# Softmax weights divided ahead of their transpose with the values stationary, and the MLP's centring and first products in high and low parts

## The chip, the core and the metric

The kernel runs on one core of a Trainium2 chip. The metric is the time on the device from start to end of one execution, in microseconds (us), as the median of several runs. The engines that matter are TensorE (matmuls and transposes; its weight loads run beside them), VectorE, ScalarE, GpSimd, and SyncE, which issues DMAs. Each engine takes its instructions strictly in the order in which they are written for it. They wait for one another only through semaphores.

## The reference

Three blocks in a row, each on a layer norm of `x` (4 sequences of 512 tokens, 128 features): softmax attention A, a two-layer block with local attention and an MLP (`ffn`), a linear attention B, and `ffn` again. The change lies in `ffn`. Cut to what matters:

```python
def _layer(x, wqkv, qs, ksc, wo, lg, lb, w1, b1, w2, b2):
    h = shift_token(x)                       # the upper 64 features come from the token before
    q, k, v = jnp.split(h @ wqkv, 3, axis=-1)   # 8 heads of 64
    q = l2norm(q) * qs
    k = l2norm(k) * ksc
    q, k = rotary_xpos(q, k)
    o = local_attention(q, k, v)             # windows of 64; each looks at itself and the one before
    x = x + o @ wo
    h = shift_token(x)
    mu = h.mean(-1, keepdims=True)
    var = h.var(-1, keepdims=True)
    h = (h - mu) / jnp.sqrt(var + 1e-05) * lg + lb
    h = h @ w1 + b1
    a, g = jnp.split(h, 2, axis=-1)          # 341 each
    h = a * jax.nn.gelu(g, approximate=False)
    return x + h @ w2 + b2
...
x = x + attn_a(_layernorm(x)); x = x + ffn(_layernorm(x)); x = x + attn_b(_layernorm(x)); x = x + ffn(_layernorm(x))
```

## The kernel before

Attention A is a program of its own (`attention_a`, the first 249 us). All that follows is `stream`: one pipeline over 64 tiles of 128 tokens (2 calls of `ffn`, 2 layers, 4 sequences, 4 tiles each). Four tiles make a group, that is one sequence in one layer; there are 16 groups.

The order on each engine is written out by the table `STEP`. In step s an engine goes through its list, and a stage with lag L works on tile s - L in that step (`of_tile`), or on a group once in four steps (`of_group`), or on a sequence of attention B between the two calls (`of_sequence`). So a row's place in the list and its lag decide what stands ahead of what. The four steps of a group hold different group work: after the group's last tile, wo comes 3 steps later, the centring and the variance 4, w1 5, w2 6. So each of the four steps of a group has one of these. On TensorE the centring and w1 stand ahead of the masks of the scores, the variance, w2 and wo behind them.

For one tile, in the order of the data: `project` (TensorE, L1157 to L1159: q, k and v, each as three products of high and low parts in the type fp32r); `squares` (ScalarE, L1368); `rope` (VectorE, four operations at L1521 and L1525 into `A` and `BS`, then the reduction of the squares, L1532); `norm` (ScalarE) and `scale` (GpSimd, L1086 and L1091); `turn` (TensorE transposes q and k, L1167) and its copies (ScalarE, L1388 and L1392); `scores` (TensorE, masks at L1180, products at L1195); the row maxima (VectorE, `soften`, L1557); the exponentials (ScalarE, `soften`, eight of 128x128 into `PW`, L1402); `turn_p` (TensorE, transposes of `PW`, L1205) and the two copies into `PT` (one on ScalarE, L1424, one on VectorE, L1549); `sums` (TensorE, L1216): the transposed weights stand still and the values `V` and `VS`, with a column of ones for the sum of the weights, are moved through; the division (VectorE, L1564 and L1568, into `ON`); `turn_o` (TensorE, transposes of `ON`, L1228) and its copy into `OT` (ScalarE, L1433). Then, once a group: `wo` (TensorE, L1255; VectorE adds at L1574; GpSimd shifts into `mid`, L1106 to L1110), the centring (L1273) and the variance (L1279) as FP32 products on TensorE with ScalarE's square, logarithm and exponential (L1446, L1453, L1456) and VectorE's two operations into `mid` (L1583, L1587), `w1` (TensorE, six FP32 products, L1286; ScalarE's gelu; VectorE at L1603), `w2` (TensorE, L1294; VectorE at L1613, or L1620 and L1624).

The 8 banks of PSUM go round in the order in which TensorE's stages take them: `take(kind, i)` waits until the bank's occupant of eight places earlier has been read (`FREED`).

Of the kernel before, what the change touches and what calls it, by code (L numbers as in the profile page):

```python
# [858 lines left out]
def of_first(k):  # L859
# [6 lines left out]
           ("project", 0, of_tile), ("features_b", 10, of_sequence), ("turn", 1, of_tile), ("context", 9, of_sequence),  # L866
           ("turn_o", 3, of_tile), ("project_b", 10, of_sequence), ("w1", 5, of_group), ("turn_p", 2, of_tile), ("turn_p_2", 2, of_tile),
# [3 lines left out]
           ("var_y", 10, of_sequence), ("w2", 6, of_group), ("wo", 3, of_group), ("sums", 2, of_tile), ("store", 6, of_end)],  # L871
    "ACT": [("features_a", 0, of_first), ("latent", 8, of_sequence),
            ("squares", 0, of_tile), ("features_b", 10, of_sequence), ("turn", 1, of_tile), ("values", 0, of_tile), ("turn_o", 3, of_tile),
            ("center_mlp", 4, of_group), ("center_a", 2, of_first), ("center_b", 7, of_sequence),
            ("center_y", 10, of_sequence), ("split", SEQS, of_tile), ("w1", 5, of_group), ("turn_p", 2, of_tile), ("keys_b", 8, of_sequence),
            ("norm", 0, of_tile), ("var_mlp", 4, of_group), ("var_a", 2, of_first), ("var_b", 7, of_sequence),
            ("var_y", 10, of_sequence), ("soften", 1, of_tile), ("store", 6, of_end)],
    "DVE": [("lead", 0, of_lead), ("project_a", 1, of_first), ("latent", 8, of_sequence), ("rope", 0, of_tile), ("context", 9, of_sequence), ("project_b", 10, of_sequence),
            ("w1", 5, of_group), ("turn_p_2", 2, of_tile), ("keys_b", 8, of_sequence), ("soften", 1, of_tile),
            ("tokens_b", 9, of_sequence), ("var_mlp", 4, of_group), ("var_a", 2, of_first),  # L880
            ("var_b", 7, of_sequence), ("var_y", 10, of_sequence), ("wo", 3, of_group),
            ("w2", 6, of_group), ("sums", 2, of_tile)],
    "POOL": [("lead", 0, of_lead), ("split", SEQS, of_tile), ("scale", 0, of_tile), ("w2", 6, of_group),
# [23 lines left out]
def stream(nc, a, g, out):  # L907

    psum, X, Y, eps, cst, cstb = g.psum, g.X, g.Y, g.eps, g.cst, g.cstb
    norms, number = number_norms()  # L910

    order = []
    for stage, i in engine_plan("PE"):
# [4 lines left out]
        elif stage in ("scores", "sums", "keys_b", "tokens_b"):  # L918
# [5 lines left out]
        elif stage == "latent":  # L924
            order += [("latent", i), ("query_b", i)]
        elif stage[:7] == "center_":
            order += [("center", number[stage[7:], i])]
        elif stage[:4] == "var_":
            order += [("var", number[stage[4:], i])]
        elif stage in ("turn_o", "wo", "w2", "context", "features_b", "project_b", "store", "features_a", "project_a"):  # L930
            order += [(stage, i)]
    at = {x: i for i, x in enumerate(order)}

    def bank(kind, i):
# [7 lines left out]
             "sums": ("divided", lambda i: i + 1), "turn_o": ("o_copied", lambda i: i + 1),  # L942
# [17 lines left out]
    with ExitStack() as ctx:  # L960
# [8 lines left out]
        w1 = sb("w1", [P, LAYERS, 2 * HID])  # L969
# [14 lines left out]
        V = sb("V", [P, 4, HW, DW + 1])  # L984
        VS = sb("VS", [P, 4, HW, DW + 1])
# [3 lines left out]
        RD = sb("RD", [P, 4, PAIRS])  # L989
        ON = sb("ON", [P, 4, PAIRS, DW])  # L990
        OT = sb("OT", [P, PAIRS, T])
        mid = sb("mid", [P, T])
        ln_squared = sb("ln_squared", [P, T])
        LR = sb("LR", [P, T])
        gates = sb("gates", [P, 3, T])
        hidden = sb("hidden", [P, 3, T])
# [11 lines left out]
        OUT = sb("OUT", [P, 2, 4, P])  # L1008

        def pieces():  # L1010

            todo = []
            for layer in range(LAYERS):
                def row(name):
                    return a[name][layer:layer + 1]

                by_head = row("L0_ffn_wo").rearrange("a (cc c j d) n -> c d (a cc) j n", cc=2, c=2, j=2)
                todo += [
                    *((wo[DW * c:DW * c + DW, layer, 2 * cc:2 * cc + 2, :], by_head[c, :, cc])
                      for c in range(2) for cc in range(2)),  # L1020
# [16 lines left out]
        with block:  # L1037
            @block.sync
            def _(sp):
# [3 lines left out]
                sp.wait_ge(s("zeroed"), 3)  # L1043
                for stage, k in engine_plan("SP"):
                    if stage == "values":

                        sp.wait_ge(s("v_copied"), k + 1)
                        if k >= 4:
                            sp.wait_ge(s("sums"), 2 * k - 6)
# [15 lines left out]
            def _(pool):  # L1065
                nc.gpsimd.memset(KT[:, :, 2 * TILES - 1, :], 0.0).then_inc(s("zeroed"), 1)
                nc.gpsimd.memset(VS[0:WIN, :, :, :], 0.0).then_inc(s("zeroed"), 1)
                nc.gpsimd.memset(V[:, :, :, DW:DW + 1], 1.0).then_inc(s("zeroed"), 1)
# [4 lines left out]
                nc.gpsimd.memset(mid[64:P, 0:1], 0.0).then_inc(s("mid_zero"), 1)  # L1073
                pool.wait_ge(s("mid_zero"), 1)
# [7 lines left out]
                for stage, i in engine_plan("POOL"):  # L1082
                    if stage == "scale":
# [8 lines left out]
                            .then_inc(s("scaled"), 1)  # L1092
# [611 lines left out]
```

## Time and profile before

| | before |
|---|---|
| median of 3 runs | 1003.37 us (1003.19 to 1005.01) |
| the profiled execution | 1004.09 us, of it the span of the core 1002.3 us |
| TensorE busy (weight loads apart) | 941.9 us, 94% |
| VectorE, ScalarE busy | 737.2 us, 74%; 730.1 us, 73% |
| GpSimd busy | 384.0 us, 38% |
| granted TensorE clock, mean | 0.991 |

The busy times are sums over the whole span, and matmuls overlap one another in the records, so that a start-to-start distance tells more of their price than a duration does. Idle time is shown with what ended it. A wait for several semaphores is put down to the last. The granted clock is given as a share of full speed, so that 0.50 is the lower level.

### The profile page before, as it was taken

The numbers are of one execution on the slowest core, as the hardware profiler recorded it, in microseconds if no ns is written. First come the engines' busy times: TensorE is split into PE (matmuls) and PEld (weight loads), VectorE is DVE, ScalarE is ACT, GpSimd is POOL, SyncE is SP. The second block draws the span as 40 slices with busy tenths as digits, with TensorE's granted clock in tenths as the row PEclk, the third lists the DMA queues.
The fourth block names the chain that finished last, engine by engine and source line by source line (L and its number), as shares of the span: only waits on it lengthen the run. The fifth ranks groups of instructions, "written<-read, shape, count | busy, mean of one in ns | idle before, by whom it ended". The sixth has DMA issues, their size and how long they took to land.

```text
span 1002.3 us, 22947 instructions
## 1 busy us (share of the span) xinstructions
PE 941.9 (94%) x8744; PEld 577.3 (58%) x8744; DVE 737.2 (74%) x1225; ACT 730.1 (73%) x1564; POOL 384.0 (38%) x266
## 2 busy tenths in 40 slices
PE   8999999998889999999999999999999999999985
PEld 4333333333566676666766566666666766667652
DVE  6887878883887777777777677777677777777741
ACT  3577777777687786877867677777777868788652
POOL 2110113101666535455443534444365354544501
PEclk9999999999899999999999999999999999999997
DMA  2200000000411101011000101000011010110100
GB/s 82 66 8 2 2 1 2 2 1 2 122 29 28 24 18 33 18 28 23 18 23 17 23 18 23 17 17 18 18 27 24 18 33 18 27 35 17 44 12 10
DMA packets 23303, 23.72 MB, mean 24 GB/s; under 512 B 8626, under 2 KB 15068, under 8 KB 23196
## 3 DMA queue, kind: packets, MB, share of 16 engines
q1 hardware_dynamic: 23196, 22.27, 9.3%
q8 instruction: 71, 1.16, 0.5%
q14 instruction: 36, 0.29, 0.1%
HBM read 6.16 MB, written 1.05 MB: 7 GB/s over the span
## 4 chain that ended last, share of the span: by engine, by line
PE 54%; DVE 11%; ACT 5%; issue 3%; POOL 2%; DVEq 0%; POOLq 0%
PE psum L1286 8%; PE psum L1255 6%; PE psum L1195 5%; PE psum L1294 4%; PE psum L1216 4%; PE psum L1205 3%; PE psum L1167 3%; PE psum L1157 3%; DVE f_BS L1525 3%; PE psum L1279 3%; DVE f_A L1521 3%; PE psum L1159 3%; PE psum L1158 3%; PE psum L1273 2%; PE psum L1180 2%
## 5 line engine op out<-in xcount | busy, mean ns | idle before, releaser
L1086 POOL TENSOR_TENSOR f_A<-f_A,f_BS 128x1024 f32<-128x1024 f32 x64 | 151.1, 2362 | 201.1 <-DVE f_BS L1525 200.9
L765 DVE TENSOR_REDUCE a_M<-psum 128x2 f32<-128x1024 f32 x128 | 155.4, 1221 | 33.4 <-PE psum L560 32.6
L1091 POOL TENSOR_TENSOR f_A<-f_A,f_RN 128x1024 f32<-128x1024 f32 x64 | 121.8, 1903 | 90.0 <-ACT f_RN L1417 86.1
L1402 ACT ACTIVATE f_PW<-psum,f_NM 128x128 f32<-128x128 f32 x512 | 138.9, 382 | 16.4 <-DVE f_NM L1557 16.4
L683 ACT ACTIVATE a_PT<-psum 128x1024 f32<-128x1024 f32 x128 | 128.6, 1023 | 23.5 <-PE psum L570 23.4
L1521 DVE TENSOR_TENSOR f_A<-psum,cos 128x512 f32<-128x512 f32 x128 | 87.7, 685 | 37.7 <-ACT f_SQ L1368 37.6
L1368 ACT ACTIVATE f_SQ<-psum 128x512 f32<-128x512 f32 x128 | 74.5, 624 | 49.7 <-PE psum L1159 46.8
L1557 DVE TENSOR_REDUCE f_NM<-psum 128x4 f32<-128x512 f32 x128 | 82.2, 684 | 32.7 <-PE psum L1195 32.7
L1286 PE MATMUL psum<-f_mid,f_w 128*128 128x512 f32 (+1 forms) x192 | 87.4, 605 | 2.7 <-DVE f_mid L1587 2.7
L1525 DVE TENSOR_TENSOR f_BS<-psum,sin 128x512 f32<-128x512 f32 x128 | 87.2, 681 | 0.0
L1216 PEld LDWEIGHTS psum<-f_VS,f_PT 128*64 128x64 f32 x1024 | 64.5, 137 | 38.8 <-issue 37.5
L492 PE MATMUL psum<-a_PT,a_VA 128*12 128x256 f32 x1024 | 79.4, 383 | 0.2 <-ACT a_PT L683 0.2
L1532 DVE TENSOR_REDUCE f_SS<-f_SQ 128x16 f32<-128x1024 f32 x64 | 77.4, 1209 | 0.0
L1216 PE MATMUL psum<-f_VS,f_PT 128*64 128x65 f32 x1024 | 73.3, 225 | 0.7 <-DMA f_VS<-f_V 0.5
L1167 PE MATMUL psum<-const,f_A 128*128 128x128 f32 x512 | 66.6, 273 | 7.4 <-POOL f_A L1091 7.4
L1216 PE MATMUL psum<-f_V,f_PT 128*64 128x65 f32 x1024 | 73.3, 225 | 0.0
L1167 PEld LDWEIGHTS psum<-const,f_A 128*128 128x128 f32 x512 | 59.3, 140 | 17.0 <-POOL f_A L1091 9.5
L1195 PE MATMUL psum<-f_KT,f_QT 64*64 64x128 f32 x2048 | 68.2, 271 | 0.4 <-ACT f_KT L1392 0.4
L1205 PE MATMUL psum<-const,f_PW 128*128 128x128 f32 x512 | 67.1, 273 | 1.0 <-DVE f_BS L1525 1.0
L1205 PEld LDWEIGHTS psum<-const,f_PW 128*128 128x128 f32 x512 | 58.5, 141 | 12.4 <-issue 12.4
L1216 PEld LDWEIGHTS psum<-f_V,f_PT 128*64 128x64 f32 x1024 | 64.5, 137 | 0.0
L1195 PEld LDWEIGHTS psum<-f_KT,f_QT 64*64 64x64 f32 x2048 | 61.6, 134 | 4.8 <-ACT f_KT L1392 0.7
(196 smaller groups left out, 1936.2 us busy)
## 6 DMA issues: line engine op xcount, KB each, us to landing
f_VS<-f_V SPq DMA_DIRECT2D x112, 130.0 KB, 2.3
raw<-L_ffn_wqkv_dram SPq DMA_DIRECT2D x2, 768.0 KB, 5.8
a_XT<-L_attn_a_x_dram SPq DMA_DIRECT2D x4, 256.0 KB, 2.9
out_dram<-f_OUT SPq DMA_DIRECT2D x4, 256.0 KB, 2.3
f_w<-L_ffn_w_dram SPq DMA_DIRECT2D x2, 341.0 KB
tables<-const_dram SPq DMA_DIRECT2D x1, 512.0 KB, 3.7
f_wo<-L_ffn_wo_dram SPq DMA_DIRECT2D x8, 64.0 KB
const<-const_dram SPq DMA_DIRECT2D x1, 264.0 KB, 3.0
```

Of the source, the lines that this page charges most:

```text
L683: nc.scalar.activation(PT[:, i % 4, :, :], psum[:, pair("by_key", i), :], ACT.Exp, scale=float(DA) ** -0.5).then_inc(s("exped"), 1)
L765: nc.vector.tensor_reduce(M[:, quads % 2, t, 2 * j:2 * j + 2], psum[:, pair("scores", i), :], AX_X, ALU.max).then_inc(s("maxed"), 1)
L1086: nc.gpsimd.tensor_tensor(A[:, k % 2, :, :], A[:, k % 2, :, :], BS[:, k % 2, :, :], ALU.add)\
L1091: nc.gpsimd.tensor_tensor(x, x, RN[:, k % 2, :, None].to_broadcast([P, 2 * HW, DW]), ALU.mult)\
L1167: last = nc.tensor.transpose(dst[:, P * c:P * c + P], A[:, k % 2, w, P * c:P * c + P], g.ident)
L1195: last = nc.tensor.matmul(dst[j][WIN * w:WIN * w + WIN, P * c:P * c + P].rearrange("p (s x) -> p s x", s=2), QT[rows, k % 2, c, WIN * w:WI ...
L1205: last = nc.tensor.transpose(dst[:, P * c:P * c + P], PW[:, u % 4, c, :], g.ident)
L1216: last = nc.tensor.matmul(dst[WIN * w:WIN * w + WIN, c, :], PT[:, u % 4, c, WIN * w:WIN * w + WIN], values[:, k % 4, 2 * c + j, :], start= ...
L1286: nc.tensor.matmul(take(kind, 3 * i + blk)[0:w, :], w1[:, layer, first + lo:first + lo + w], mid[:, :], start=True, stop=True).then_inc(s( ...
L1402: last = nc.scalar.activation(PW[:, u % 4, c, :], psum[:, bank("scores", u), P * c:P * c + P], ACT.Exp, bias=NM[:, u % 4, c:c + 1])
L1521: nc.vector.tensor_tensor(A[:, k % 2, w, :].rearrange("p (h d) -> p h d", d=DW), x.rearrange("p (h d) -> p h d", d=DW), g.cos[:, layer, t, ...
L1525: nc.vector.tensor_tensor(BS[:, k % 2, w, :].rearrange("p (h s d) -> p h s d", s=2, d=DW // 2), x.rearrange("p (h s d) -> p h s d", s=2, d ...
```

## The change

There are two parts that do not depend on each other.

**Attention.** The exponentials in `PW` are summed by VectorE (a reduction over each 128, both halves of the tile at once), the reciprocals are taken, and GpSimd multiplies `PW` by them: the new stage `weigh`, lag 2, ahead of `rope` on VectorE and of `scale` on GpSimd. The transposes `turn_p` wait for that and go from lag 2 to 3, one ahead of `turn` and one behind it. In `sums` the values now stand still and the weights are moved through, so that the result comes out transposed: the ones column, the division on VectorE, `ON` and `turn_o` go, and ScalarE copies the result of `sums` straight into `OT`. `sums` has lag 3 and stands ahead of the centring and of `scores`, where before it was the last stage but one of a step. The copy L1549 on VectorE keeps its place behind `rope`, with lag 3.

**MLP.** `mid` becomes a high part `mid_h` and a low part `mid_l` (fp32r). GpSimd makes both; the centring is two products in place of one FP32 product; each of the six first products is three. VectorE makes the two parts of the normalized input with one more operation. The weights w1 and the centring matrix are split once, at step 4 on ScalarE (`split_w1`) and step 5 on GpSimd. `wo` is loaded in another layout, in 2 transfers in place of 8.

```diff
-           ("turn_o", 3, of_tile), ("project_b", 10, of_sequence), ("w1", 5, of_group), ("turn_p", 2, of_tile), ("turn_p_2", 2, of_tile),
+           ("project", 0, of_tile), ("features_b", 10, of_sequence), ("turn_p", 3, of_tile), ("turn", 1, of_tile), ("context", 9, of_sequence),
+           ("turn_p_2", 3, of_tile), ("project_b", 10, of_sequence), ("w1", 5, of_group), ("sums", 3, of_tile),
...
+    "DVE": [("lead", 0, of_lead), ("project_a", 1, of_first), ("latent", 8, of_sequence), ("weigh", 2, of_tile), ("rope", 0, of_tile), ("turn_p_2", 3, of_tile),
...
+                    elif stage == "weigh":
+                        k = i
+                        pool.wait_ge(s("den_recip"), k + 1)
+                        x = PW[:, 2 * (k % 2):2 * (k % 2) + 2, :, :].rearrange("p u c x -> p (u c) x")
+                        nc.gpsimd.tensor_tensor(x, x, RD[:, k % 2, :, None].to_broadcast([P, 2 * PAIRS, P]), ALU.mult)\
+                            .then_inc(s("weighed"), 1)
...
                 def turn_p(u):
-                    pe.wait_ge(s("exped"), u + 1)
+                    pe.wait_ge(s("weighed"), u // 2 + 1)
...
                 def sums(k):
                     pe.wait_ge(s(f"moved{k % 4}"), moved(k))
-                    for j in range(2):
-                        u = 2 * k + j
-                        pe.wait_ge(s(("p_copied", "p_copied_2")[j]), k + 1)
...
-                                    dst[WIN * w:WIN * w + WIN, c, :], PT[:, u % 4, c, WIN * w:WIN * w + WIN],
-                                    values[:, k % 4, 2 * c + j, :], start=True, stop=True)
...
+                    pe.wait_ge(s("v_copied"), k + 1)
+                    dst = take("sums", k).rearrange("p (c x) -> p c x", c=PAIRS)
+                    pe.wait_ge(s("p_copied"), k + 1)
+                    pe.wait_ge(s("p_copied_2"), k + 1)
+                    for c in range(PAIRS):
+                        for w, values in ((0, VS), (1, V)):
+                            for j in range(2):
                                 last = nc.tensor.matmul(
+                                    dst[DW * j:DW * j + DW, c, WIN * w:WIN * w + WIN],
+                                    values[:, k % 4, 2 * c + j, :],
+                                    PT[:, (2 * k + j) % 4, c, WIN * w:WIN * w + WIN], start=True, stop=True)
+                    last.then_inc(s("sums"), 1)
...
+                        if use == "mlp":
+                            nc.tensor.matmul(dst, centre[:, :], mid_h[:, :], start=True, stop=False)
+                            last = nc.tensor.matmul(dst, centre[:, :], mid_l[:, :], start=False, stop=True)
...
+                                nc.tensor.matmul(dst, w1_h[:, layer, of], mid_h[:, :], start=True, stop=False)
+                                nc.tensor.matmul(dst, w1_h[:, layer, of], mid_l[:, :], start=False, stop=False)
+                                nc.tensor.matmul(dst, w1_l[:, layer, of], mid_h[:, :], start=False, stop=True)\
+                                  .then_inc(s(kind), 1)
...
+                    elif stage == "weigh":
+                        k = i
+                        dve.wait_ge(s("exped"), 2 * k + 2)
+                        if k >= 2:
+                            dve.wait_ge(s("weighed"), k - 1)
+                        x = PW[:, 2 * (k % 2):2 * (k % 2) + 2, :, :].rearrange("p u c x -> p (u c) x")
+                        nc.vector.tensor_reduce(RD[:, k % 2, :], x, AX_X, ALU.add).then_inc(s("den"), 1)
+                        dve.wait_ge(s("den"), k + 1)
+                        nc.vector.reciprocal(RD[:, k % 2, :], RD[:, k % 2, :]).then_inc(s("den_recip"), 1)
...
+                            nc.vector.scalar_tensor_tensor(out=mid_l[:, :], in0=ln_squared[:, :],
+                                                           scalar=vecs[:, layer, 1:2], in1=mid_h[:, :].bitcast(F32),
+                                                           op0=ALU.add, op1=ALU.subtract).then_inc(s("ln_done"), 1)
```

What this does to the order, on VectorE first, between the maxima (`f_NM`) of one tile and those of the next, in a step of wo. Before:

```order
L1557 TENSOR_REDUCE f_NM<-psum 128x4 x2
L1574 TENSOR_TENSOR Y<-Y,psum 128x512
L1564 RECIPROCAL f_RD<-psum 128x4
L1568 TENSOR_TENSOR f_ON<-psum,f_RD 128x256
L1564 RECIPROCAL f_RD<-psum 128x4
L1568 TENSOR_TENSOR f_ON<-psum,f_RD 128x256
L1521 TENSOR_TENSOR f_A<-psum,cos 128x512
L1525 TENSOR_TENSOR f_BS<-psum,sin 128x512
L1521 TENSOR_TENSOR f_A<-psum,cos 128x512
L1525 TENSOR_TENSOR f_BS<-psum,sin 128x512
L1532 TENSOR_REDUCE f_SS<-f_SQ 128x16
L1549 COPY f_PT<-psum 128x512
```

And the same stretch of the changed kernel (its L1577 is the old L1557, L1592 the old L1574, L1569 the old L1549):

```order
L1577 TENSOR_REDUCE f_NM<-psum 128x4 x2
L1592 TENSOR_TENSOR Y<-Y,psum 128x512
L1586 TENSOR_REDUCE f_RD<-f_PW 128x8
L1588 RECIPROCAL f_RD<-f_RD 128x8
L1541 TENSOR_TENSOR f_A<-psum,cos 128x512
L1545 TENSOR_TENSOR f_BS<-psum,sin 128x512
L1541 TENSOR_TENSOR f_A<-psum,cos 128x512
L1545 TENSOR_TENSOR f_BS<-psum,sin 128x512
L1552 TENSOR_REDUCE f_SS<-f_SQ 128x16
L1569 COPY f_PT<-psum 128x512
```

The division of a tile that TensorE has already summed is replaced by the reduction of the exponentials (`f_PW`) of the very tile whose maxima stand two rows above.

On TensorE, in a step of the centring, from the end of `project` to the end of `scores`. Before, with the sums (L1216) behind this stretch:

```order
L1159 MATMUL psum<-w_h,HL 128x512
L1167 MATMUL psum<-const,f_A 128x128 x8
L1228 MATMUL psum<-const,f_ON 128x128 x4
L1205 MATMUL psum<-const,f_PW 128x128 x8
L1273 MATMUL psum<-f_mid,const 128x512
L1180 MATMUL psum<-constb 64x512 x4
L1195 MATMUL psum<-f_KT,f_QT 64x128 x16
L1279 MATMUL psum<-f_ln_squared,const 128x512
```

And in the changed kernel (L1230 are the sums, L1193 and L1208 the scores); of the sums the last two rows of eight stand here:

```order
L1218 MATMUL psum<-const,f_PW 128x128 x4
L1180 MATMUL psum<-const,f_A 128x128 x8
L1218 MATMUL psum<-const,f_PW 128x128 x4
...
L1230 MATMUL psum<-f_PT,f_VS 64x64 x2
L1230 MATMUL psum<-f_PT,f_V 64x64 x2
L1277 MATMUL psum<-f_mid_h,f_centre 128x512
L1278 MATMUL psum<-f_mid_l,f_centre 128x512
L1193 MATMUL psum<-constb 64x512 x4
L1208 MATMUL psum<-f_KT,f_QT 64x128 x16
```

`turn_o` (L1228) is gone, and `sums`, which needs both copies into `PT`, has come to stand ahead of the scores.

## Rows read from the trace of the kernel before

**Rows 1.** Busy time in stretches: length, then us (instructions) by engine, clock, DMA, GB/s.
```profile
455.50:497.30 41.80, 40.72 (x423) 28.64 (x419) 32.29 (x58) 32.59 (x81) 22.00 (x15) 1.00 0.11 24
533.40:587.70 54.30, 51.73 (x460) 34.40 (x461) 39.72 (x74) 39.45 (x95) 23.19 (x16) 1.00 0.08 19
```
**Rows 2.** Timeline of TensorE, start us, duration us, line, tiles, count, [idle before].
```profile
460.69 0.41 PE L1180 MATMUL psum<-constb 64*64 64x512 bf16 x4 [0.64 <-DVE f_BS L1525]
...
470.74 0.41 PE L1180 MATMUL psum<-constb 64*64 64x512 bf16 x4 [0.43 <-DVE f_BS L1525]
...
476.67 0.50 PE L1157 MATMUL psum<-f_qkv_h,HH 128*128 128x512 f32 x1
...
478.87 1.04 PE L1167 MATMUL psum<-const,f_A 128*128 128x128 f32 x8
479.74 0.60 PE L1228 MATMUL psum<-const,f_ON 128*128 128x128 f32 x4
480.18 1.04 PE L1205 MATMUL psum<-const,f_PW 128*128 128x128 f32 x8
481.05 1.02 PE L1273 MATMUL psum<-f_mid,const 128*128 128x512 f32 x2
482.01 0.41 PE L1180 MATMUL psum<-constb 64*64 64x512 bf16 x4
```
**Rows 3.** Pieces of the chain that ended last: start us, us, what, count.
```profile
475.65 1.08 PE psum L1216 x32
...
489.03 5.15 PE psum L1286 x12
```
**Rows 4.** Timeline of VectorE over the same steps.
```profile
464.79 1.53 DVE L1620 SCALAR_TENSOR_TENSOR HH<-psum,f_vecs,Y 64x512 fp32r<-64x512 f32 x2 [1.32 <-PE psum L1294]
...
467.02 0.17 DVE L1564 RECIPROCAL f_RD<-psum 128x4 f32<-128x4 f32 x1
...
468.12 0.68 DVE L1521 TENSOR_TENSOR f_A<-psum,cos 128x512 f32<-128x512 f32 x1
...
471.64 0.68 DVE L1549 COPY f_PT<-psum 128x512 f32<-128x512 f32 x1
472.23 1.28 DVE L1557 TENSOR_REDUCE f_NM<-psum 128x4 f32<-128x512 f32 x2
475.69 0.69 DVE L1574 TENSOR_TENSOR Y<-Y,psum 128x512 f32<-128x512 f32 x1 [2.18 <-PE psum L1255]
...
483.37 1.29 DVE L1557 TENSOR_REDUCE f_NM<-psum 128x4 f32<-128x512 f32 x2 [0.79 <-PE psum L1195]
485.77 0.75 DVE L1583 SCALAR_TENSOR_TENSOR f_mid<-psum,f_vecs,f_LR 128x512 f32<-128x512 f32 x1 [1.11 <-ACT f_LR L1456]
```
**Rows 5.** Timeline of ScalarE: the exponentials after wo and after the variance.
```profile
472.95 2.18 ACT L1402 ACTIVATE f_PW<-psum,f_NM 128x128 f32<-128x128 f32 x8 [0.30 <-DVE f_NM L1557]
...
485.64 2.16 ACT L1402 ACTIVATE f_PW<-psum,f_NM 128x128 f32<-128x128 f32 x8
```
**Rows 6.** Groups by line, whole span: count, busy us, mean ns, idle before.
```profile
L1532 DVE TENSOR_REDUCE f_SS<-f_SQ 128x16 f32<-128x1024 f32 x64 | 77.4, 1209 | 0.0
L1091 POOL TENSOR_TENSOR f_A<-f_A,f_RN 128x1024 f32<-128x1024 f32 x64 | 121.8, 1903 | 90.0 <-ACT f_RN L1417 86.1
```
**Rows 7.** Timeline of TensorE where it had stood idle.
```profile
258.64 1.09 PE L1167 MATMUL psum<-const,f_A 128*128 128x128 f32 x8 [2.34 <-POOL f_A L1091]
...
260.47 1.98 PE L1195 MATMUL psum<-f_KT,f_QT 64*64 64x128 f32 x32 [0.40 <-ACT f_KT L1392]
...
301.16 1.09 PE L1167 MATMUL psum<-const,f_A 128*128 128x128 f32 x8 [1.76 <-POOL f_A L1091]
...
986.56 7.49 PE L1286 MATMUL psum<-f_mid,f_w 128*128 128x512 f32 x12 [2.75 <-DVE f_mid L1587]
```
**Rows 8.** Stretches of 4 us, columns as in rows 1; the last but two is the clock.
```profile
260.00:264.00 4.00, 3.60 (x40) 2.93 (x37) 4.00 (x7) 1.64 (x5) 3.12 (x3) 0.57 0.62 164
299.00:303.00 4.00, 2.24 (x19) 1.85 (x18) 3.61 (x5) 1.82 (x5) 1.96 (x2) 1.00 0.00 0
```

## What the change does to the time, predicted before it ran

> **What bounds the kernel now.** I read the busy time by stretch first: a group of four tiles takes 41.8 us with TensorE busy for 40.7, and a group that also carries attention B takes 54.3 us with 51.7 [rows 1]. Twelve groups of the first kind and four of the second lie behind attention A. VectorE and ScalarE are busy for 32.3 and 32.6 us of the 41.8. The timelines show why three engines that are so full hardly wait: VectorE's maxima (L1557) follow its copy (L1549) at once, 471.64 and 472.23 [rows 4], since TensorE had issued the scores at 470.74 [rows 2], and all that needs VectorE's copy or ScalarE's exponentials is a step away. So I looked for the change not in the sums of work but in the loop of waits that its order makes.
>
> **The work that it takes from TensorE.** Pitches come from starts in [rows 2]: nine products of high and low parts 2.20 us (476.67 to 478.87), so 0.24 each; `turn_o` 0.44; `turn_p` 0.87; one FP32 centring 0.96. `turn_o` goes: 64 x 0.44 = 28 us. The first products of the MLP go from 5.15 us [rows 3] to 18 x 0.24 = 4.3: 16 x 0.85 = 14 us. The MLP's centring goes from 0.96 to 0.48: 8 us. The weighted sums keep their 16 matmuls of 64 columns, 1.08 us a tile [rows 3]; which operand stands still costs nothing. Together 50 us.
>
> **What it adds.** VectorE loses four small operations on PSUM a tile (467.02 to 468.12, 1.10 us [rows 4]) and gets a reduction over 128x1024, like L1532 at 1.21 us, and a reciprocal, 0.14: `weigh` takes 1.35. Per group comes `mid_l`, taken like the operation at 485.77, 0.75 busy. GpSimd gets one product of 128x1024 a tile like L1091, 1.90 us [rows 6], and per group a low part in place of a memset, some 2.5 us; at 22 us busy of 41.8 [rows 1] it has the room. By work alone nothing here eats the 50 us.
>
> **The order is what costs.** Call M the moment at which TensorE issues the masks (L1180) of a step. In the new order VectorE runs maxima(k-1), weigh(k-1), rope(k+1), copy(k-2), and only then the next maxima. weigh needs all of ScalarE's exponentials of the tile whose maxima were just made; TensorE's `sums`, now ahead of `scores`, needs the copy that lies behind rope; the maxima need the scores. That is a closed loop with one tile in it:
> - masks to maxima 1.36 (482.01 [rows 2], 483.37 [rows 4]);
> - maxima to the first exponential 0.72 (472.23 [rows 4], 472.95 [rows 5]), eight of them 2.18 [rows 5], handing over 0.04: 2.94;
> - weigh 1.35;
> - rope and its reduction 3.52 (468.12 to 471.64 [rows 4]);
> - copy and hand-over, 0.68 + 0.12: 0.80;
> - sums 1.08, then the masks again.
>
> Together 11.05 us, even where no group work lies in it: that is the stretch from the masks of w1's step to those of w2's, called plain below, in which TensorE has 6.2 us to do. In 41.8 us there are four steps of 10.45 on the mean, group work included.
>
> Group work then lengthens the loop where it stands in it. After w2 VectorE's three writes start at M + 4.10 and end at M + 6.33 (460.69 [rows 2]; 464.79, 467.02 [rows 4]) where the exponentials are ready at M + 4.3: 13.1 us; in the last layer one write, 11.5; mean 12.3. After wo the addition starts at M + 4.95 (470.74; 475.69) and takes 0.63; with the two centring products: 12.8. In the step of the variance ScalarE's exponentials start only at M + 3.63 (482.01; 485.64 [rows 5]) and end at 5.84; then weigh 1.35, half of rope (1.2) and only then is the bank of q free for the first `up`: the banks rotate by eight, so five products of 0.72 follow the rope one by one; sums start at M + 12.5: 13.6. The plain stretch 11.0. Sum 49.7: **7.9 us more** per group. For the groups with attention B I walked the same loop with its operations added where they stand (centring and keys on TensorE ahead of the scores, queries, tokens and the norm on VectorE ahead of weigh): 58.8 against 54.3, 4.5 more, the least certain term (0 to 12).
>
> **The clock.** In that loop TensorE stands still between its last transpose and `sums`. From M it has scores 1.2, project 2.2 and transposes 1.74: in the plain stretch it is idle from 5.1 to 10.0, 4.8 us; after w2 4.2 or 2.6; after wo 2.5; ahead of and within w1 never over 1.6. The trace shows what such idling does: after 2.34 us idle the next four microseconds ran at a granted 0.57, mostly at the lower of the two levels, 1.2 GHz, and the scores took 1.98 us in place of 1.04; after 2.75 idle (with an earlier drop) the MLP's twelve took 7.49, against 5.15; after 1.76 idle it stayed 1.00 [rows 3, 7, 8]. So I expect a fall in three of four steps. It hits the TensorE part of the loop, sums (+1.1) and masks to maxima (+1.1): 2.2 us each, 1.3 for the fall after the shortest idle: 5.7 per group; about 6 where B is. Nothing (if it doesn't fall) to 8 are the bounds.
>
> The Trainium skill ("TensorE: Matmul & The Clock Gate", HAM oscillation) tells of a kernel whose clock fell anew at every tile through a wait between short bursts, and reckons half of the throttled time as lost. With some 3.6 us throttled per fall that would be an estimate of 1.8 us for each in place of 2.2; this trace agrees on the fall and has too few of them to decide on the size.
>
> **Sum.** The first group has no full loop yet and is left as it is. 11 x (7.9 + 5.7) = 150; 4 x (4.5 + 6) = 42; the end gets 4 (low parts on GpSimd and VectorE, in a chain that nothing covers). The split of w1 and the fewer weight transfers lie beside the start's work: 0, at most 5. 196 us on the profiled execution's 1004.1 gives 1200, and the median is 0.7 lower: **1199 us**. The 50 us that TensorE saves are inside its idle time and give nothing.
>
> **Rivals.**
> 1. The clock holds, or falls seldom. The loop alone stands: 87 + 18 + 4 over 1003: **1112 us**. For it: a cold TensorE is itself less idle, and each idle is cut by work of other stages. Against it: idles here are longer than any that the trace bears at full clock. Chance 0.17.
> 2. The other side: **faster, 955 to 1000**. TensorE was the bound, 97% busy in a group, and is given 50 us. It needs VectorE to find exponentials ready when it comes to weigh, so that weigh costs its 1.35 us and no wait; that decides below a loop of 10.4 us. Taking all hand-overs as nothing brings the loop only to 10.7, so one term must be misread, for instance weigh working on the tile before. Chance 0.07; the same time as before within it is 0.01.
> 3. The loop is there but partly loosened, B's groups being fully covered by the new idle time: 1020 to 1095. Chance 0.08.
> 4. More: every fall costs the whole loop, GpSimd falls behind (scale is ready only 0.3 to 0.9 us ahead of its turn in the steps after wo), so that the turns come late too: 1240 to 1280. Chance 0.10.
>
> **How the numbers follow.** The main case, 0.58, spans 1150 to 1235. Range: 1105 to 1240, which takes in rival 1 and leaves out some 0.2. A measurement of this kernel can tell about 0.2%, 2 us, from no change. Faster by more 0.06, within 0.01, slower 0.93.
>
> **What would show it.** In the new trace: VectorE's reduction for the weights waits some 1.7 us for ScalarE's exponentials in a plain stretch, and its maxima wait some 2.6 us for the scores; TensorE waits for VectorE's copy ahead of `sums`, 2.5 to 4.9 us, in three steps of four; a group without B takes 55 us (49.7 at full clock); the granted clock over such a group is 0.75 to 0.85. VectorE's busy share falls to about 60%, TensorE's matmul work, if the clock held, to 38 us a group. Wrong would be the prediction if the exponentials are there first, or if TensorE gets to the scores without waiting for the copy; too high, if the granted clock stays at 1.00; and the term for the loop is wrong if a plain stretch does not come to 11.0 us at full clock.

## The result

| | before | after |
|---|---|---|
| median | 1003.51 us (1003.19 to 1005.01) | 1213.41 us (1210.01 to 1216.95) |
| ratio | | 1.2084, 95% interval 1.2053 to 1.2115 |
| the profiled execution, of it the span | 1004.09, 1002.3 us | 1210.82, 1209.0 us |
| granted TensorE clock, mean | 0.991 | 0.915 |

The changed kernel is 21% slower. The prediction was 1199 us, in a range of 1105 to 1240. First the page of the changed kernel: busy time by engine, two lines of its span in 40 slices, and three groups of instructions (count | busy us, mean ns of one | idle time just before them and what ended most of it).

```profile
PE 970.5 (80%) x8584; PEld 621.9 (51%) x8584; DVE 764.1 (63%) x1113; ACT 729.7 (60%) x1566; POOL 549.8 (45%) x378
...
PE   8999999976677777777788887878777777877875
...
PEclk9999999988788888898889899989899898999897
...
L1230 PE MATMUL psum<-f_PT,f_VS 128*64 128x64 f32 x1024 | 89.9, 274 | 168.5 <-DVE f_PT L1569 168.5
L1577 DVE TENSOR_REDUCE f_NM<-psum 128x4 f32<-128x512 f32 x128 | 82.4, 685 | 210.1 <-PE psum L1208 210.1
...
L1586 DVE TENSOR_REDUCE f_RD<-f_PW 128x8 f32<-128x1024 f32 x64 | 77.7, 1214 | 25.0 <-ACT f_PW L1414 25.0
```

No engine is full any more. TensorE waits 168.5 us ahead of `sums` (L1230) for VectorE's copy of the turned weights (L1569), and VectorE waits 210.1 us ahead of its maxima (L1577) for TensorE's scores (L1208). Each waits for the other, which is what a closed loop looks like in a page. From the end of attention A on, TensorE's busy digits are mostly 7 and 8.

Next the stretches. Here are the four steps of one group (from TensorE's masks, L1193, to the next masks: after w2, after wo, the step of w1, plain), then two whole groups, without and with attention B. The columns are those of [rows 1].

```profile
478.55:493.90 15.35, 11.23 (x105) 8.38 (x107) 8.95 (x13) 6.75 (x18) 8.47 (x5) 0.83 0.08 19
493.90:508.80 14.90, 12.42 (x108) 8.71 (x107) 7.39 (x11) 6.75 (x18) 10.06 (x9) 0.84 0.09 19
508.80:522.60 13.80, 12.16 (x118) 8.72 (x121) 10.84 (x16) 12.47 (x26) 6.21 (x3) 1.00 0.05 10
522.60:534.26 11.66, 7.01 (x94) 5.99 (x93) 6.79 (x10) 6.66 (x19) 6.14 (x3) 0.93 0.11 24
...
478.55:534.26 55.71, 42.82 (x410) 31.80 (x408) 33.98 (x50) 32.62 (x80) 30.88 (x20) 0.90 0.08 18
655.01:719.97 64.96, 53.61 (x451) 36.46 (x450) 41.09 (x66) 38.98 (x93) 33.36 (x22) 0.92 0.07 15
```

A group that took 41.80 us [rows 1] takes 55.71. VectorE and ScalarE are busy in it for 33.98 and 32.62 us, against 32.29 and 32.59 before: 1.7 us more on VectorE and none on ScalarE. GpSimd has 8.9 us more (30.88 against 22.00) but is busy for only 55% of the group. So the 13.9 us are not work that was added to a full engine. The clock is below 1.00 in three of the four steps; in that of w1 it is 1.00 here. In two of the three TensorE stands idle ahead of the sums as follows, and in the third for 4.65 us at 532.51.

```profile
491.95 0.48 PE L1230 MATMUL psum<-f_PT,f_VS 128*64 128x64 f32 x4 [4.12 <-DVE f_PT L1569]
...
505.72 0.49 PE L1230 MATMUL psum<-f_PT,f_VS 128*64 128x64 f32 x4 [2.48 <-DVE f_PT L1569]
```

From the starts of all masks in both traces the 206.7 us between the profiled executions can be placed. "Ten groups" are those without attention B that have a whole neighbour on both sides.

| part of the span | before | after | more |
|---|---|---|---|
| first group (while the pipeline fills) | 34.8 | 49.9 | 15.1 |
| ten groups without B | 418.6 | 556.3 | 137.7 |
| four groups with B | 216.3 | 255.0 | 38.7 |
| last group, three steps | 33.8 | 41.2 | 7.4 |
| start and end | | | some 8 |

Last the loop itself, in a plain step: the timeline from one set of masks to the next and on to the next maxima.

```profile
579.31 0.41 PE L1193 MATMUL psum<-constb 64*64 64x512 bf16 x4
579.55 1.04 PE L1208 MATMUL psum<-f_KT,f_QT 64*64 64x128 f32 x32
...
580.67 1.29 DVE L1577 TENSOR_REDUCE f_NM<-psum 128x4 f32<-128x512 f32 x2 [1.51 <-PE psum L1208]
...
581.39 2.17 ACT L1414 ACTIVATE f_PW<-psum,f_NM 128x128 f32<-128x128 f32 x8 [0.38 <-DVE f_NM L1577]
...
583.59 1.22 DVE L1586 TENSOR_REDUCE f_RD<-f_PW 128x8 f32<-128x1024 f32 x1 [1.64 <-ACT f_PW L1414]
...
584.85 0.20 DVE L1588 RECIPROCAL f_RD<-f_RD 128x8 f32<-128x8 f32 x1
584.97 0.65 DVE L1541 TENSOR_TENSOR f_A<-psum,cos 128x512 f32<-128x512 f32 x1
...
588.46 0.68 DVE L1569 COPY f_PT<-psum 128x512 f32<-128x512 f32 x1
589.28 0.48 PE L1230 MATMUL psum<-f_PT,f_VS 128*64 128x64 f32 x4 [4.65 <-DVE f_PT L1569]
589.52 0.45 PE L1230 MATMUL psum<-f_PT,f_V 128*64 128x64 f32 x4
...
591.18 0.64 PE L1193 MATMUL psum<-constb 64*64 64x512 bf16 x4
...
591.61 1.92 PE L1208 MATMUL psum<-f_KT,f_QT 64*64 64x128 f32 x32
...
593.61 1.29 DVE L1577 TENSOR_REDUCE f_NM<-psum 128x4 f32<-128x512 f32 x2 [4.48 <-PE psum L1208]
```

Each stage waits for the one above it: masks to maxima 1.36, maxima to the end of the exponentials 2.92 (580.67 to 583.59), weigh 1.38 (to 584.97), rope and its reduction 3.49 (to 588.46), the copy 0.82 (to 589.28), sums 1.90 (to 591.18). All but the last are the prediction's terms to within 0.03. The sums take 1.90 in place of 1.08 and the scores 1.92 in place of 1.04, since TensorE stood idle for 4.65 us and then ran at the lower level, 1.2 GHz. Two stretches of 4 us in the trace show it: 0.67 from 586 to 590, 0.50 from 590 to 594.

```profile
586.00:590.00 4.00, 0.72 (x14) 0.75 (x16) 3.13 (x5) 0.48 (x1) 3.37 (x2) 0.67 0.30 66
590.00:594.00 4.00, 4.00 (x61) 3.32 (x58) 0.39 (x1) 1.31 (x4) 1.25 (x1) 0.50 0.01 4
```

### The profile page after: what moved, and what is told of

Read it like the earlier page. It is cut to its first block, busy times and chain, and to the rows that moved or that the text cites. A ratio compares the mean times of both kernels' runs of the same rounds, so it can differ in the third digit from the quotient of the medians.

```text
span 1209.0 us, 22493 instructions
## 1 busy us (share of the span) xinstructions
PE 970.5 (80%) x8584; PEld 621.9 (51%) x8584; DVE 764.1 (63%) x1113; ACT 729.7 (60%) x1566; POOL 549.8 (45%) x378
## 4 chain that ended last, share of the span: by engine, by line
PE 36%; DVE 25%; ACT 9%; issue 8%; POOL 0%; ACTq 0%; DVEq 0%
PE psum L1230 8%; PE psum L1208 6%; DVE f_BS L1545 5%; PE psum L1256 5%; DVE f_RD L1586 5%; ACT f_PW L1414 4%; DVE f_SS L1552 4%; DVE f_A L1541 4%; PE psum L1306 3%; DVE f_PT L1569 3%; PE psum L1193 2%; PE psum L1286 2%; PE psum L1297 2%; PE psum L1298 1%; PE psum L1299 1%
## 5 line engine op out<-in xcount | busy, mean ns | idle before, releaser
L1230 PE MATMUL psum<-f_PT,f_VS 128*64 128x64 f32 x1024 | 89.9, 274 | 168.5 <-DVE f_PT L1569 168.5
L1577 DVE TENSOR_REDUCE f_NM<-psum 128x4 f32<-128x512 f32 x128 | 82.4, 685 | 210.1 <-PE psum L1208 210.1
L1230 PEld LDWEIGHTS psum<-f_PT,f_VS 128*64 128x64 f32 x1024 | 74.3, 180 | 187.0 <-issue 187.0
L1096 POOL TENSOR_TENSOR f_PW<-f_PW,f_RD 128x1024 f32<-128x1024 f32 x64 | 121.4, 1896 | 105.7 <-DVE f_RD L1588 104.0
L1445 ACT ACTIVATE f_OT<-psum 128x512 f32<-128x512 f32 x64 | 38.1, 595 | 119.3 <-PE psum L1230 119.1
L1586 DVE TENSOR_REDUCE f_RD<-f_PW 128x8 f32<-128x1024 f32 x64 | 77.7, 1214 | 25.0 <-ACT f_PW L1414 25.0
L1208 PE MATMUL psum<-f_KT,f_QT 64*64 64x128 f32 x2048 | 89.4, 329 | 0.4 <-ACT f_KT L1404 0.4
L1230 PE MATMUL psum<-f_PT,f_V 128*64 128x64 f32 x1024 | 88.8, 270 | 0.0
L1208 PEld LDWEIGHTS psum<-f_KT,f_QT 64*64 64x64 f32 x2048 | 82.3, 174 | 9.1 <-issue 6.1
L1460 ACT ACTIVATE f_ln_squared<-psum 128x512 f32<-128x512 f32 x25 | 14.9, 598 | 119.4 <-PE psum L1278 78.5
L1218 PE MATMUL psum<-const,f_PW 128*128 128x128 f32 x512 | 76.8, 273 | 1.8 <-ACT f_PW L1414 1.8
L1230 PEld LDWEIGHTS psum<-f_PT,f_V 128*64 128x64 f32 x1024 | 76.3, 184 | 0.0
```

Source lines behind the costliest of these rows:

```text
L1096: nc.gpsimd.tensor_tensor(x, x, RD[:, k % 2, :, None].to_broadcast([P, 2 * PAIRS, P]), ALU.mult)\
L1208: last = nc.tensor.matmul(dst[j][WIN * w:WIN * w + WIN, P * c:P * c + P].rearrange("p (s x) -> p s x", s=2), QT[rows, k % 2, c, WIN * w:WI ...
L1230: last = nc.tensor.matmul(dst[DW * j:DW * j + DW, c, WIN * w:WIN * w + WIN], values[:, k % 4, 2 * c + j, :], PT[:, (2 * k + j) % 4, c, WIN ...
L1586: nc.vector.tensor_reduce(RD[:, k % 2, :], x, AX_X, ALU.add).then_inc(s("den"), 1)
```

## The experiments

### Which half of the change costs

The two parts do not depend on each other, so each was built alone. `attn_only` is the changed kernel with the FP32 MLP of before; `mlp_only` is the kernel before with the high and low parts in centring and w1, and with attention as it was.

> The changed kernel with the MLP as it was before (one FP32 centring product, six FP32 first products of 0.86 us, one mid). Theory: TensorE's 22 us of added work lie partly in the loop, since w1's products follow the banks that rope frees and the centring stands between sums and scores: +0.7 and +0.5 us a group, so 1213 + 19 = 1232 us, 1215 to 1245. Rival (the MLP's part is to blame for some of the 210 us): clearly below 1213.

Measured 1227.82 us, ratio 1.2229 (1.2205 to 1.2253), as expected.

> The kernel before with the MLP's part of the change alone (mid in high and low parts, two centring products, three first products for each one, the split of w1; two small buffers share memory to make room); attention as before, with turn_o and the old order. Theory (before, TensorE is the bound at 97% of a group, and its work counts there): 22 us less, 981 us, at least half of it after waits: 975 to 992. Rival (the MLP's part itself costs, through GpSimd's low parts of 2.5 us a group and VectorE's extra operation): 1003 or more.

Measured 996.11 us, ratio 0.9919 (0.9893 to 0.9945): 0.8% faster than before, and the fastest kernel of this study, but a miss: 8 us in place of 22, and outside the range of 975 to 992. Its two groups:

```profile
422.35:463.26 40.91, 39.86 (x424) 29.57 (x425) 32.75 (x59) 32.58 (x81) 23.47 (x17) 1.00 0.11 25
609.28:662.23 52.95, 50.37 (x467) 35.44 (x466) 40.35 (x74) 39.25 (x93) 25.96 (x18) 1.00 0.09 19
```

Where TensorE is the bound, nearly all of what it is spared comes through: its busy time falls by 0.86 us a group and the group by 0.89 (40.91 against 41.80 [rows 1]). What fell short is the busy time spared, as 22 us would be 1.4 a group. Over the 16 groups of the profiled execution 13.3 us are gained; the end is 2.5 us longer, and attention A, which this kernel does not change, 5.2 us longer at a granted clock of 0.96 where it was 0.99. The attention part, then, costs 224 us (1227.8 against 1003.9), and the MLP part gives back 8 on the old order and 14 on the new one (1227.8 against 1213.4).

### Is the slow clock a cost of its own

`warm` gives TensorE something to do while it waits: three FP32 products whose result the sums overwrite.

```diff
                     pe.wait_ge(s("p_copied"), k + 1)
+                    for _ in range(3):
+                        nc.tensor.matmul(psum[:, bank("sums", k), :], g.ident, g.const[:, 0:T], start=True, stop=True)
                     pe.wait_ge(s("p_copied_2"), k + 1)
```

> The changed kernel with three FP32 products of 512 constant columns (2.6 us at full clock) issued ahead of each wait of `sums` for VectorE's copy; they write the bank that `sums` then overwrites, and nothing reads them. Theory (a closed loop, and on top of it a clock that falls in TensorE's idle time and makes sums and scores slow): the clock stays near 1.00 in the stream and the time falls by the clock's term, 5.7 us a group, to 1120 to 1150 us. Rival (the low clock only shows the idling and costs nothing, since TensorE is not the bound): 1213 us or more by the extra work where the idle time is short.

Measured 1188.11 us, ratio 1.184 (1.1788 to 1.1892), clock 0.987: a miss. The plain stretch became exactly 11.0, those after w2 and wo 13.0 each, but the step of w1 went from 13.8 or 14.9 to 16.3: there TensorE has no idle time ahead of the sums, and the filler came on top. So `warm2` leaves it out in that step alone (`range(0 if k >= 5 and k % 4 == 1 else 3)`).

> The changed kernel with three FP32 products of 128x512 ahead of the wait for VectorE's copy of the weights, as in the run before it, but left out in the step of w1, where TensorE has no idle time to fill. Loop-and-clock theory: the clock stays near 1.00 and the groups without attention B come to 50.5 us or a little less (13.0, 13.0, 13.6 to 14, 11.0), so that the whole takes 1143 us (1130 to 1155): 70 us of the changed kernel's 210 belong to the clock and 140 to the loop. Rival (the clock costs nothing of its own, because a faster TensorE only waits longer): 1185 us or more, as with the filler in all steps.

Measured 1151.94 us, ratio 1.1476 (1.1448 to 1.1505), clock 0.987.

```profile
456.33:507.06 50.73, 45.90 (x431) 30.97 (x428) 33.99 (x50) 32.63 (x80) 30.90 (x20) 1.00 0.09 20
680.25:742.30 62.05, 57.64 (x469) 36.87 (x468) 41.10 (x66) 38.99 (x93) 33.41 (x22) 1.00 0.07 16
```

A group at full clock takes 50.73 us, in steps of 13.0, 13.0, 13.7 and 11.0. The clock is thus worth at least 61 us of the 210 (1213.4 less 1151.9), and the loop some 149 or less. "At least", because the filler is not free in every step: with B it made the plain stretch 13.4 where it was 12.3, at full clock both times.

### Does the loop follow its terms

`half_reduce` sums only every second exponential (`x[:, :, ::2]`), so half of the terms of each denominator are left out; all else stays. It shortens one term of the loop, the reduction, from 1.21 to 0.68 us.

> The changed kernel whose VectorE reduction in `weigh` takes every second exponential, 512 elements in place of 1024 (so half of each sum is left out). Theory (weigh lies in the closed loop of every tile): 64 x 0.53 us less, 34 us, so 1179 us. Rival (VectorE is 63% busy and its work is covered): 1213 us.

Measured 1191.15 us, ratio 1.187 (1.1823 to 1.1917): 22 us less than the changed kernel, where the loop theory wanted 34. Plain stretches fell from 11.8 to 11.3, nearly all of it; those after w2 and wo by some 0.3 each on the mean of ten groups; the step of w1 by less than 0.1. Where the clock stays at 1.00 in both, the steps of w1 show the gain too. These are the steps of w1 and of the plain stretch in the one group of `half_reduce` without B that has both at full clock:

```profile
859.12:872.34 13.22, 12.10 (x114) 8.67 (x113) 10.38 (x16) 12.30 (x26) 8.06 (x4) 1.00 0.05 11
872.34:882.87 10.53, 6.41 (x98) 5.44 (x95) 6.26 (x10) 6.73 (x19) 6.14 (x3) 1.00 0.12 26
```

The first took 13.75 in the changed kernel at full clock, 0.53 more, and with B the plain stretch fell from 12.27 to 11.74 and the step of w1 from 16.03 to 15.5. So an operation of VectorE, an engine that is 63% busy, sets the time of these steps one for one. In the other groups of `half_reduce` the clock fell in the step of w1 (0.91 to 0.94, and 0.87 in the first of them) and took the gain back there; its mean over the span is 0.907, against 0.915. Why it fell there is not shown.

### What opens the loop

Four more orders of the same stages were tried, to see which hand-over must leave it. `weigh_late` puts weigh behind the copy on VectorE, and behind `scale` on GpSimd:

```diff
-    "DVE": [..., ("weigh", 2, of_tile), ("rope", 0, of_tile), ("turn_p_2", 3, of_tile),
+    "DVE": [..., ("rope", 0, of_tile), ("turn_p_2", 3, of_tile), ("weigh", 2, of_tile),
-    "POOL": [..., ("weigh", 2, of_tile), ("scale", 0, of_tile), ...
+    "POOL": [..., ("scale", 0, of_tile), ("weigh", 2, of_tile), ...
```

> The changed kernel with `weigh` moved behind rope and the copy on VectorE, and behind `scale` on GpSimd; nothing else. Theory: the exponentials leave the loop, what is left is rope 3.5, copy 0.8, sums 1.1, scores to maxima 1.4, maxima 1.3; a group falls from 49.7 to some 43 us at full clock, against 41.8 of before: 1005 to 1075 us, the upper end if the clock still falls in the idle time of 2 us that is left. Rival (the loop is not what costs; GpSimd's added work or the low parts are): over 1150 us.

Measured 1149.13 us, ratio 1.1451 (1.1407 to 1.1496): 64 us better than the changed kernel and far from the expectation. Its waits (us in total, times, longest):

```profile
DVE f_NM L1577 <- PE psum L1208: 118.3, 59, 4.1
...
PE psum L1230 <- DVE f_PT L1569: 98.2, 48, 3.6
...
PE psum L1218 <- POOL f_PW L1096: 38.7, 28, 3.0
```

The exponentials are no longer waited for by rope, but copy, sums, masks, maxima, rope and copy still close a loop, and a new wait stands beside it: TensorE's transposes (L1218) for GpSimd's product (L1096), which now stands behind a `scale` that waits for ScalarE's norm. The clock still falls, 0.939 over the span.

`copy_first` puts the copy ahead of rope on VectorE and both transposes ahead of those of q and k on TensorE:

```diff
-    "DVE": [..., ("weigh", 2, of_tile), ("rope", 0, of_tile), ("turn_p_2", 3, of_tile),
+    "DVE": [..., ("weigh", 2, of_tile), ("turn_p_2", 3, of_tile), ("rope", 0, of_tile),
-    "PE": [..., ("turn_p", 3, of_tile), ("turn", 1, of_tile), ..., ("turn_p_2", 3, of_tile),
+    "PE": [..., ("turn_p", 3, of_tile), ("turn_p_2", 3, of_tile), ("turn", 1, of_tile), ...
```

> The changed kernel with both `turn_p` ahead of `turn` on TensorE and the copy L1569 ahead of rope (behind weigh) on VectorE. Theory: rope leaves the loop between weigh and sums and the masks then wait for the banks of q and k only: 8.8 us in the plain stretch in place of 11.0, some 43.3 us a group, TensorE's idle stretches under 1.8 us, so that the clock holds: 1010 to 1050 us. Rival (the exponentials alone close the loop whatever follows them): 1180 us or more.

Measured 1092.85 us, ratio 1.0891 (1.0801 to 1.098). The plain stretch is 8.9, as forecast; the whole is 43 us above the range. The step of w1 is what is long: 15.1 to 17.1 us in the ten groups. With the banks taken in another order, the second product of w1 finds the bank that it needs still held by rope:

```profile
423.59 0.50 PE L1297 MATMUL psum<-f_mid_h,f_w_h 128*128 128x512 f32 x1
...
426.72 0.51 PE L1297 MATMUL psum<-f_mid_h,f_w_h 128*128 128x512 f32 x1 [2.16 <-DVE f_BS L1545]
...
428.98 0.63 PE L1297 MATMUL psum<-f_mid_h,f_w_h 128*128 128x512 f32 x1
```

Some 1.7 us after the end of this wait the products began to run slow: the fourth one starts at 428.98 with 0.63 in place of 0.50. That the bank makes this step long is read from the trace; no run tests it in this order.

`sums_last` moves TensorE's `sums` to the end of its step, behind scores and the group work, so that neither the scores nor the maxima wait for the copy; both `turn_p` stand behind `turn`, and `wo`, all after it and attention B go one step later. `sums_last_weigh_late` also has weigh behind the copy.

```diff
-    "PE": [..., ("w1", 5, of_group), ("sums", 3, of_tile), ..., ("scores", 1, of_tile), ..., ("wo", 3, of_group), ...
+    "PE": [..., ("w1", 6, of_group), ..., ("scores", 1, of_tile), ..., ("wo", 4, of_group), ("sums", 3, of_tile), ...
```

> The changed kernel with `sums` moved from ahead of the scores to the end of the step on TensorE, its ScalarE copy one step later, wo, centring, w1, w2 and all of attention B each one step later so that they still find their data, and both turn_p behind turn; weigh still ahead of rope. Theory: TensorE's scores no longer wait for VectorE's copy; the loop left is maxima 1.3 with exponentials 2.9, weigh 1.35, rope 3.5, copy 0.6, so 8.4 us in the plain stretch and some 41 us a group: 985 to 1010 us. Rival (moving weigh matters, moving sums does not): 1150 us or more.

> As sums_last, and weigh behind the copy on VectorE and behind scale on GpSimd. Theory: no loop is left that is longer than the work; TensorE's 36.7 us of a group and VectorE's 34 set the time, some 39 us a group against 41.8 of before: 945 to 975 us. Rival (GpSimd's chain weigh, turn_p, or the weights' longer way closes another loop): 1000 us or more.

Measured 1077.07 us, ratio 1.0711 (1.068 to 1.0742), and 1074.64 us, ratio 1.0704 (1.0674 to 1.0734). Both missed: they are 67 and 100 us above their ranges. The ratios' intervals overlap: once `sums` stands last, the place of weigh no longer decides. Three of the four stretches are now short (7.2 to 8.8, 10.0, 11.6), but that of w1 is 15.3. From the trace of the second:

```profile
428.01 0.69 ACT L1445 ACTIVATE f_OT<-psum 128x512 f32<-128x512 f32 x1
...
428.85 0.47 PE L1297 MATMUL psum<-f_mid_h,f_w_h 128*128 128x512 f32 x1 [1.39 <-ACT f_OT L1445]
...
433.30 1.28 ACT L1483 ACT_TABLE_LOAD   x1
434.60 0.60 ACT L1436 ACTIVATE f_PT<-psum 128x512 f32<-128x512 f32 x1
...
435.25 0.41 PE L1193 MATMUL psum<-constb 64*64 64x512 bf16 x4 [1.99 <-ACT f_PT L1436]
```

The first product of w1 waits for a bank that ScalarE's copy of the sums frees, and the masks wait for one that its copy of the weights frees, which stands behind three GELUs and two table loads. `copies_early` takes that order and moves the two copies on ScalarE:

```diff
-            ("squares", 0, of_tile), ..., ("turn", 1, of_tile), ("values", 0, of_tile), ("sums", 4, of_tile),
+            ("sums", 4, of_tile), ("squares", 0, of_tile), ..., ("turn", 1, of_tile), ("turn_p", 3, of_tile), ("values", 0, of_tile),
-            ..., ("w1", 6, of_group), ("turn_p", 3, of_tile), ...
+            ..., ("w1", 6, of_group), ...
```

> The order with the sums at the end of TensorE's row and the weights divided behind the copy, with ScalarE's two copies out of PSUM (sums and turned weights) moved from behind the GELUs to ahead of them. Bank theory: in the former order w1's stretch is 15.3 us because the first product of w1 waits 1.39 us for a bank that ScalarE's copy of the sums frees and the masks wait 1.99 us for the copy of the weights behind the GELUs and two table loads. With both gone the stretch falls to 12 to 12.5 us, groups without attention B to 40.5 to 42, the whole from 1075 to 1025 us (1010 to 1040). Rival (the stretch is long because of rope's products and the variance, whatever the banks do): 1065 us or more.

Measured 1040.95 us, ratio 1.0358 (1.0341 to 1.0375): 34 us less than the order that it mends, one us above the range that was given, 16 above its middle value. Its groups:

```profile
343.26:384.80 41.54, 38.60 (x409) 27.70 (x408) 34.51 (x52) 31.96 (x81) 30.79 (x20) 1.00 0.11 24
620.10:677.91 57.81, 52.02 (x451) 35.87 (x450) 42.97 (x67) 38.85 (x94) 33.54 (x22) 0.94 0.08 17
```

The bank theory holds in the main: the two waits were what made w1's stretch long. In eight of the ten groups without B it is 12.4 to 13.9 now (forecast 12 to 12.5), and these take 41.5 to 43.1, near the 41.8 of before. So 172 of the 210 us were order alone, with every instruction of the change in place. Of the 37 us that are left in the profiled executions, 8 lie in B's groups (57.8 against 54.3 [rows 1] in three of the four), 11 in the group behind them (54.3 against 43.5), 8 in the first two groups, 7 in the last group and the end together, one step longer, and 3 in the other eight. TensorE's busy time in a group is 38.60 at full clock, where 40.72 stood before; even here that saving is not turned into time. Whether an order exists that does so was not found.

## Why the prediction was right

**The loop.** It was put at 11.05 us for a plain step at full clock and is 11.0 in `warm` and `warm2`. Without a filler, `half_reduce` has 10.53 at full clock for a loop that is 0.53 shorter. The other stretches were put at 13.1 (after w2, with three writes), 12.8 (after wo) and 13.6 (w1); `warm2` has 13.0, 13.0 and 13.7. The waits that were to show it are there: the reduction waits 1.64 us for the exponentials (forecast 1.7), the sums 4.12, 2.48 and 4.65 in three steps of four (forecast 2.5 to 4.9), none in w1's. The maxima's wait, forecast at 2.6, is 1.51 in the plain step shown, as VectorE's last product with the gates of w1 (578.41 to 579.16) fills part of it.

**The step that failed: the mean of 12.3 after w2.** It took half of the groups as having one write of w2 in place of three, and such a step as 11.5 us long. Both were wrong. In the traces eight of the ten groups without B carry the writes of a first layer, one carries none, and only one the single write of a last layer; those of the first call's last layer fall into B's groups. And with the single write the step is 13.0 us in `warm2`, as with the others (13.3 in the changed kernel, begun cold): ScalarE's copy of the output delays its squares, and rope waits for them.

```profile
1074.65 0.69 DVE L1541 TENSOR_TENSOR f_A<-psum,cos 128x512 f32<-128x512 f32 x1 [0.79 <-ACT f_SQ L1380]
```

Of the loop term, 7.9 us a group, 0.8 is missing: it should have been 8.7, and `warm2` shows 8.9 in a steady group (50.73 less 41.80).

**The clock.** Where it falls was right: at the sums in the plain step, after w2 and after wo, not at the short waits for banks in w1's (1.23 to 1.25 us). The first of the ten groups is the exception: there that wait was 2.03 us, and the clock fell 1.6 us behind it. Its size was the second term that was wrong. Ten groups sum to 556.3 us in the changed kernel and to 510.7 in `warm2`, 4.5 us a group in place of 5.7. The fall after the shortest wait is not a sure one: of 2.47 or 2.48 us each time, it was followed by sums at the lower level in five groups, came only behind the sums in three (see below), and in two not at all. The granted clock over a group was to be 0.75 to 0.85 and is 0.89 over the ten. With 28 falls in those ten groups, one costs 1.6 us, where the prediction counted 2.2 for the longer ones.

The Trainium skill ("TensorE: Matmul & The Clock Gate", HAM oscillation) counts half of the throttled time as lost. The estimate of 1.8 us a fall that was made with it came near only because it took 3.6 us as throttled: in the trace the ten groups have 125.6 us at the lower level (a mean clock of 0.887 over 556.3 us), 4.5 a fall, and half of that is 2.2. Less is lost here, as part of the low time lies in TensorE's idle time: from 586 to 590, with the clock at 0.67, TensorE is busy for 0.72 us of 4.

The two errors cancel, which is luck: 13.6 us more a group were forecast and 13.8 measured, where the right loop with the forecast clock would have given 14.6.

**Attention B.** Forecast 10.5 us a group, 42 in all; measured 38.7. The split was off: at full clock, with its filler, the four sum to 246.6 us, 7.6 a group above before. Some 1.1 of that is filler (its plain stretch), which leaves 6.5 for the loop, put at 4.5, and 3.2 for the clock, put at 6.

**The first group and the ends.** "The first group has no full loop yet and is left as it is" was wrong: it went from 34.8 to 49.9 us, as its second stretch is already 14.8 us long. The loop needs one tile in weigh and one in sums, and these are there from that stretch on. The sum gave 196 us for the profiled execution and 206.7 were measured, 11 short: the first group is 15 of it, and the ten groups 2, while B's groups gave 3 less than forecast and the last group with both ends 15 in place of 18 (one group's 13.6 and 4). That the median is short by 14 comes from the profiled execution, which is 2.6 us below the median here and was 0.7 above it before.

**TensorE's saving.** It was to "give nothing", and was the smaller error: 14 us of it, the MLP's, came through (`attn_only` less the changed kernel), since that work stands in the loop. In the profiled executions w1's step at full clock is 14.41 us in `attn_only` and 13.75 in the changed kernel, and the stretches after wo, where the centring stands between the sums and the masks, are 1.0 us longer on the mean of ten. Its work in a group was put at 38 at full clock and is 38.60 in `copies_early`.

**The rivals.** That the clock holds (1112 us) fell with the clock's 0.915; its size was short as well, since `warm2` takes 1152. That of a faster kernel needed weigh to find the exponentials ready, which it does not: it waits for them. `sums_last_weigh_late` shows that even with this removed the time stays above before. The rival in which B's groups are covered fell with their 38.7 us. The one above 1240 us fell with the 1.6 us that a fall costs, and because the turns of q and k do not come late: behind the first group TensorE waits for GpSimd's scaled tile once, for 0.8 us.

## What to carry to other kernels

When a change moves a stage, write down what each engine waits for from one tile to the next and follow it until it comes back to its start: the length of that loop over the tiles in it is a bound of its own, and neither busy shares nor the work saved tell of it. Open it by moving the consumer behind work that does not need it, then look at who holds a buffer longer than before: here each opened loop showed the next wait, most often on a PSUM bank that had not yet been read. And try the halves of a change apart: one of them was a gain of 0.8% that a loss of 22% hid.

## What was not expected of the hardware

The fall can come after the wait that brings it. In one group the step after wo ended with 2.47 us idle ahead of the sums, which then began at the higher level; the clock fell behind them, 1.2 us after they had begun, just ahead of the masks that open w1's step (451.78). Timeline of TensorE, then stretches of 2 us (columns as before):

```profile
449.62 0.34 PE L1230 MATMUL psum<-f_PT,f_VS 128*64 128x64 f32 x4 [2.47 <-DVE f_PT L1569]
...
461.40 0.50 PE L1297 MATMUL psum<-f_mid_h,f_w_h 128*128 128x512 f32 x1 [1.23 <-DVE f_BS L1545]
```

```profile
448.00:450.00 2.00, 0.38 (x13) 0.41 (x15) 1.47 (x2) 0.00 (x0) 1.92 (x2) 1.00 0.43 96
450.00:452.00 2.00, 2.00 (x33) 1.28 (x32) 0.00 (x0) 0.12 (x1) 2.00 (x2) 0.70 0.16 35
452.00:454.00 2.00, 2.00 (x36) 1.53 (x32) 0.00 (x0) 1.69 (x5) 0.85 (x2) 0.50 0.00 0
...
460.00:462.00 2.00, 0.77 (x4) 0.48 (x3) 2.00 (x5) 1.98 (x5) 1.74 (x1) 1.00 0.00 0
462.00:464.00 2.00, 1.78 (x8) 1.17 (x7) 2.00 (x3) 1.99 (x3) 1.54 (x2) 1.00 0.30 66
```

That step of w1 took 14.9 us in place of 13.8. The 1.23 us idle in it, at 461.40, did not bring the clock down. Filling the long waits with useless products was worth 61 us in a kernel of 1213; the same products in the step without idle time cost 2.6 us each time they ran (16.3 against 13.7).
